# Relation layer of a fused graph network: order of layer norm, table copies, word loads and early blocks, and one-hot matrices on another engine

## The reference

```python
h = relu(layernorm(x))                        # 3125 x 128
out = h @ w_self.T
weights = einsum('rb,bio->rio', coefficients, bases)   # 16 relations from 8 bases
for r in range(16):
    msg += where(edge_type == r, h[dst] @ weights[r], 0)
out = out.at[src].add(msg)                    # 100000 edges
x = x + out
```

## Time and profile before

| | |
|---|---|
| median of 3 runs | 4468.73 us (4462.77 to 4470.12) |
| the profiled execution | 4464.81 us, of which its span 4463.1 us |
| relation layer, first instruction to end | 3338.3 to 4463.1 us |
| POOL busy | 3173.6 us (71%) |
| DVE, ACT busy | 2543.3 us (57%), 1263.6 us (28%) |
| PE busy, mean granted clock | 3091.4 us (69%), 0.686 |

### The profile page before, as it was taken

The page is one execution under the profiler, slowest core; times in us unless marked ns, Lnnn a source line. Parts: engine busy times, 40 slices in busy tenths (PEclk is TensorE's granted clock), DMA queues, the critical chain, the costliest instruction groups (busy, mean ns, idle before and its releaser), DMA issues. The chain is left out here.

```text
span 4463.1 us, 64712 instructions
## 1 busy us (share of the span) xinstructions
PE 3091.4 (69%) x17444; PEld 2321.1 (52%) x17444; DVE 2543.3 (57%) x8083; ACT 1263.6 (28%) x3878; POOL 3173.6 (71%) x3260
## 2 busy tenths in 40 slices
PE   4999999999244454454549888889878556553334
PEld 2555555556234444444448887778864333333333
DVE  6676666655456676667756666666566344431111
ACT  4333433334344444454531111111124000000000
POOL 4777777776577777777437777777764777777776
PEclk8999999999555555555555555555559787865555
DMA  4644444431334444443212223332229211211112
GB/s 98 144 94 92 94 92 94 93 87 30 105 100 108 110 106 106 106 111 103 46 46 61 74 75 79 83 88 61 56 48 283 53 52 52 53 50 50 49 49 60
DMA packets 422722, 372.59 MB, mean 83 GB/s; under 512 B 287296, under 2 KB 326090, under 8 KB 419035
## 3 DMA queue, kind: packets, MB, share of 16 engines
q0 software_dynamic: 103168, 178.48, 17.5%
q1 hardware_dynamic: 315736, 189.88, 15.7%
q10 hardware_dynamic: 3456, 0.01, 0.0%
HBM read 317.94 MB, written 35.47 MB: 79 GB/s over the span
## 5 line engine op out<-in xcount | busy, mean ns | idle before, releaser
L1108 POOL DMA_INDIRECT mlp_row<-tab,rec_d x806 | 784.5, 973 | 292.7 <-issue 244.4
L1108 POOL DMA_INDIRECT gat_row<-tab,rec_d x806 | 778.6, 966 | 265.6 <-issue 241.0
L1108 POOL DMA_INDIRECT att_row<-tab,rec_d x806 | 779.4, 967 | 255.7 <-issue 243.5
L1643 POOL DMA_INDIRECT rel_row<-tab,words_in x758 | 754.4, 995 | 231.0 <-issue 230.4
L1731 PE MATMUL rel_ps_acc<-rel_row,rel_hot 128*128 128x128 f32 x1516 | 341.7, 395 | 493.3 <-DMA rel_row<-tab,words_in 465.8
L1731 PEld LDWEIGHTS rel_ps_acc<-rel_row,rel_hot 128*128 128x128 f32 x1516 | 290.7, 285 | 618.8 <-issue 618.8
L2093 PE MATMUL gat_ps_sum<-gat_row,gat_hot 128*128 128x136 f32 x1612 | 408.3, 429 | 273.7 <-DVE gat_row L2164 250.1
L2323 PE MATMUL att_ps_sum<-att_row,att_hot 128*128 128x136 f32 x1612 | 432.8, 448 | 109.6 <-DVE acc L1485 105.1
L2093 PEld LDWEIGHTS gat_ps_sum<-gat_row,gat_hot 128*128 128x128 f32 x1612 | 352.1, 312 | 298.4 <-issue 262.8
L2323 PEld LDWEIGHTS att_ps_sum<-att_row,att_hot 128*128 128x128 f32 x1612 | 368.3, 325 | 187.1 <-DVE acc L1485 182.7
L1826 DVE TENSOR_TENSOR rel_hot<-iota,rel_local 128x512 f32<-128x512 f32 (+1 forms) x208 | 138.9, 677 | 401.0 <-PE rel_ps_acc L1731 398.0
(11 more groups left out here) (312 smaller groups left out, 5724.4 us busy)
## 6 DMA issues: line engine op xcount, KB each, us to landing
mlp_aim<-in_dst SPq DMA_DIRECT2D x195, 256.0 KB
gat_aim<-in_dst SPq DMA_DIRECT2D x195, 256.0 KB
tab<-rel_stage SPq DMA_DIRECT2D x25, 1024.0 KB, 4.8
mlp_row<-in_edge_attr SPq DMA_DIRECT2D x390, 64.0 KB, 3.0
mlp_row<-tab,rec_d POOLq DMA_INDIRECT x806
gat_row<-tab,rec_d POOLq DMA_INDIRECT x806, 2.6
att_row<-tab,rec_d POOLq DMA_INDIRECT x806
rel_row<-tab,words_in POOLq DMA_INDIRECT x758, 2.5
```

Of the source, the lines that this page charges most:

```text
L1108: gp.indirect_dma_start(row[b][:, t, :], None, table, bass.IndirectOffsetOnAxis(offsets(order[k], t), axis=0)).then_inc(s_g[b], 16)
L1643: gp.indirect_dma_start(row[r % UNROLL][:, t, :], None, tables, bass.IndirectOffsetOnAxis(g.index[:, at:at + 1], axis=0)).then_inc(s_g[r % ...
```

## The change

In neutral terms, part by part:

- **Attention bias.** `residual` no longer adds it (L887). Nine additions (`add_bias`) go in front of the extra steps of the third layer.
- **Layer norm.** DVE does the norm of all nine groups without a table copy between them. ACT copies all four parts of bins 0 to 3, and does two groups of `deviation` and `apply` behind each bin (`scaled`). From bin 4 on ACT copies parts 0 and 2, DVE parts 1 and 3. SP stores `tabh` at a = 1, 2 and 4.
- **Word loads.** SP loads run 0 at the start, runs 1 and 2 behind the stores of bins 20 and 22, and the coefficients, the bases and runs 3 to 12 behind the last store of the table.
- **Early blocks.** 16 instead of 12; the last four lie in `g.H`, and POOL waits before them until PE has transposed all groups (`s_t`).
- **Shares.** `early_coefs` runs behind the table and the first three `decode`, in two halves of 512 columns; its operand `one` lies in PSUM (`p_x`). PE waits for it (`s_mix`) before the first `chunk`, no longer for `s_in` before the products with `w_self`.
- **One-hot.** ACT makes it: a Square of (node number minus column) for each tile, and a Relu of one minus that over the block. DVE does ACT's copy to `turned`.

```diff
@@ -883,9 +883,6 @@
-            if self.layer == 3:
-                v.tensor_tensor(g.X[:, here, :], g.X[:, here, :],
-                                g.bias2[:].unsqueeze(1).broadcast_to([P, len(THREE[n]), D]), ALU.add)
@@ -1498,9 +1495,10 @@
...
-EARLY = 12
+EARLY = 16
...
+FOR_NORM = 4
@@ -1518,7 +1516,7 @@
 def by_vector(a, part):
-    return part == 3 or part == 1 and a >= len(THREE) - 2
+    return a >= FOR_NORM and part % 2 == 1
 def copies(vector, a, part):
@@ -1527,23 +1525,25 @@
     return sum(by_vector(*divmod(n, 4)) == vector for n in range(4 * a + part + 1))
-def early_coefs(v, ch, g, spare, kind_i, kind, coef, s_in):
...
+def early_coefs(v, ch, g, one, prod, kind_i, kind, coef, s_in):
+    word, most = g.word[:, 0:EARLY * TILES], EARLY * TILES // 2
+    wide = [P, most, N_REL]
+    one, prod = (x.rearrange("p (t r) -> p t r", r=N_REL) for x in (one, prod))
+    per_base = coef[:].rearrange("p (r b) -> p b r", b=N_BASES)
+    ch.do(v.tensor_scalar(kind_i[:], word, INDEX_BIT, N_REL - 1, ALU.logical_shift_right, ALU.bitwise_and))
+    ch.do(v.tensor_copy(kind[:], kind_i[:]))
+    ch.do(v.tensor_single_scalar(kind[:], kind[:], 1.0, ALU.add))
     v.wait_ge(s_in, 32)
...
+    for n in range(2):
+        here = slice(n * most, (n + 1) * most)
+        ch.do(v.tensor_tensor(one, g.iota[:, 0:N_REL].unsqueeze(1).broadcast_to(wide),
+                              kind[:, here].unsqueeze(2).broadcast_to(wide), ALU.is_equal))
+        for b in range(N_BASES):
+            ch.do(v.tensor_tensor(prod, one, per_base[:, b].unsqueeze(1).broadcast_to(wide), ALU.mult))
+            ch.do(v.tensor_reduce(g.mixes[:, here, b], prod, AX.X, ALU.add))
 def relation(nc, g, args, tables, out):
@@ -1567,15 +1567,14 @@
         number, local = c.sb("number", [P, HALF_TILES * N_HALVES], I32), c.sb("local", [P, HALF_TILES * N_HALVES])
...
-        homes = [g.TMP[:].rearrange("p a f -> p (a f)"), g.acc[:].rearrange("p a f -> p (a f)")]
-        half = EARLY // 2
-        early = [homes[o // half][:, o % half * BLOCK:(o % half + 1) * BLOCK].rearrange("p (t f) -> p t f", t=TILES)
+        homes = [home[:].rearrange("p a f -> p (a f)") for home in (g.TMP, g.acc, g.H)]
+        each = N_ROWS // BLOCK
+        early = [homes[o // each][:, o % each * BLOCK:(o % each + 1) * BLOCK].rearrange("p (t f) -> p t f", t=TILES)
                  for o in range(EARLY)]
...
@@ -1598,21 +1597,27 @@
         @block.sync
         def _(sp):
-            for n in runs:
+            def words(n):
                 sp.dma_start(*word_run(g, n)).then_inc(s_word[n], 16)
-            sp.dma_start(bases[:], args["bases"].rearrange("b i o -> i b o")).then_inc(s_in, 16)
-            sp.dma_start(coef[:], args["coefficients"].rearrange("r b -> (r b)").partition_broadcast(P)).then_inc(s_in, 16)
+            words(0)
             by_node = g.tabh.rearrange("(a n) f -> n a f", a=N_BINS)
             by_bin = tables.rearrange("(a n r) f -> a n (r f)", a=N_BINS, n=P)
             for a in range(N_BINS):
-                if a in (2, 5, 7):
-                    n = (2, 5, 7).index(a)
+                if a in (1, 2, 4):
+                    n = (1, 2, 4).index(a)
                     here = slice(THREE[3 * n][0], THREE[3 * n + 2][-1] + 1)
                     sp.wait_ge(norm.s_h, 3 * n + 3)
                     sp.dma_start(by_node[:, here, :], g.H[:, here, :]).then_inc(s_row, 16)
-                sp.wait_ge(s_mc, copies(True, a, 3))
+                ge(sp, s_mc, copies(True, a, 3))
                 sp.wait_ge(s_ma, copies(False, a, 3))
                 sp.dma_start(by_bin[a], stage[:, a % ring, :]).then_inc(s_out[a % ring], 16)
+                if a in (20, 22):
+                    words((20, 22).index(a) + 1)
+            sp.dma_start(coef[:], args["coefficients"].rearrange("r b -> (r b)").partition_broadcast(P)).then_inc(s_in, 16)
+            sp.dma_start(bases[:], args["bases"].rearrange("b i o -> i b o")).then_inc(s_in, 16)
+            for n in runs[3:]:
+                words(n)
@@ -1628,6 +1633,8 @@
             gp.wait_ge(s_node_i, 1)
             gp.wait_ge(s_row, 48)
             for o in range(EARLY):
+                if o == 2 * each:
+                    gp.wait_ge(s_t, len(THREE))
                 for t in range(TILES):
                     at = o * TILES + t
                     gp.indirect_dma_start(early[o][:, t, :], None, g.tabh,
@@ -1646,10 +1653,16 @@
         @block.scalar
         def _(act):
-            norm.deviation(act, 0)
-            norm.apply(act, 0)
-            keep_three(act, ht, p_t, 0, s_t, s_tc)
-            norm.deviation(act, 1)
+            def scaled(n):
+                if n < len(THREE):
+                    norm.deviation(act, n)
+                if 0 < n <= len(THREE):
+                    norm.apply(act, n - 1)
+            for n in range(3):
+                scaled(n)
+                if n == 1:
+                    keep_three(act, ht, p_t, 0, s_t, s_tc)
             for a in range(N_BINS):
                 if a >= ring:
                     act.wait_ge(s_out[a % ring], 16 * (a // ring))
@@ -1657,10 +1670,8 @@
                     if not by_vector(a, part):
                         act.wait_ge(s_m, banks * a + part + 1)
                         act.copy(stage[:, a % ring, part * 512:(part + 1) * 512], p_m[part]).then_inc(s_ma, 1)
-                if a + 2 < len(THREE):
-                    norm.deviation(act, a + 2)
-                if a + 1 < len(THREE):
-                    norm.apply(act, a + 1)
+                scaled(2 * a + 3)
+                scaled(2 * a + 4)
                 if a % 3 == 1 and a // 3 + 1 < len(THREE):
                     keep_three(act, ht, p_t, a // 3 + 1, s_t, s_tc)
             act.wait_ge(s_tabs, 1)
@@ -1670,11 +1681,26 @@
                     at = (2 * o + h) * HALF_TILES
                     act.dma_start(g.word[:, at:at + 1], g.words_dram[bass.ds(start, P)].rearrange("(p t) -> p t", t=1)
                                   ).then_inc(s_word[-1], 16)
-            for e in range(EARLY):
-                act.wait_ge(s_chunk, CHUNKS * e + 1)
-                if e >= 2:
-                    act.wait_ge(s_part, (CHUNKS - 1) * (e - 1))
-                act.copy(turned[:, e % 2, :], p_x[:]).then_inc(s_turned, 1)
+            def measure_gap(k):
+                o = ORDER[k]
+                ge(act, s_sum, k - (HOTS - 1))
+                act.wait_ge(s_loc, decoded(o))
+                for t in real_tiles(o):
+                    at = o * TILES + t
+                    ins = act.activation(hot[k % HOTS][:, t, :], g.iota[:], ACT.Square, scale=-1.0, bias=local[:, at:at + 1])
+                ins.then_inc(s_gap, 1)
+            def make_hot(k):
+                act.wait_ge(s_gap, k + 1)
+                there = hot[k % HOTS][:, tile_slice(ORDER[k]), :]
+                act.activation(there, there, ACT.Relu, scale=-1.0, bias=1.0).then_inc(s_hot, 1)
+            for k in range(N_BLOCKS + 1):
+                if k < N_BLOCKS:
+                    measure_gap(k)
+                if k:
+                    make_hot(k - 1)
         @block.tensor
         def _(pe):
@@ -1707,7 +1733,6 @@
             pe.wait_ge(s_mc, copies(True, N_BINS - 1, 3))
             pe.wait_ge(s_ma, copies(False, N_BINS - 1, 3))
             pe.wait_ge(s_tabs, 1)
-            pe.wait_ge(s_in, 32)
             for a in range(N_BINS):
                 pe.matmul(p_acc[:, a * D:(a + 1) * D], ht[:, a * P:(a + 1) * P], g.w_self[:],
                           start=(a % 4 == 0), stop=True, skip_group_check=True)
@@ -1751,6 +1776,9 @@
             for k in range(N_BLOCKS):
                 mm_sum(k)
+                if k == CHUNKS_AT:
+                    pe.wait_ge(s_in, 32)
+                    pe.wait_ge(s_mix, 1)
                 if 0 <= k - CHUNKS_AT < CHUNKS * EARLY:
                     chunk(k - CHUNKS_AT)
@@ -1760,29 +1788,18 @@
             v.wait_ge(s_w, 1)
             v.tensor_copy(g.w_self[:], p_m[3][:, 0:D]).then_inc(s_wc, 1)
             norm.begin(v)
-            norm.residual(v, 0)
-            norm.scan(v, 0)
-            norm.residual(v, 1)
-            norm.scales(v, 0)
-            norm.scan(v, 1)
+            for n in range(len(THREE)):
+                norm.residual(v, n)
+                if n:
+                    norm.scales(v, n - 1)
+                norm.scan(v, n)
+            norm.scales(v, len(THREE) - 1)
             v.wait_ge(s_word[0], 16)
             v.tensor_scalar(node_i[:], g.word[:, 0:EARLY * TILES], INDEX_BIT + 4, 0xFFF, ALU.logical_shift_right,
                             ALU.bitwise_and).then_inc(s_node_i, 1)
-            def tables_s():
-                yield from source_tables(v, ch, g, sort, turn, bins_f, s_cnt)
-                v.sem_inc(s_tabs, 1)
-                yield from early_coefs(v, ch, g, spare, kind_i, kind, coef, s_in)
-            later = tables_s()
+            later = source_tables(v, ch, g, sort, turn, bins_f, s_cnt)
             for a in range(N_BINS):
-                n = a + 2
```

(27 more changed lines are left out.)

20 lines of the change are left out of this document (removed).

## The result

The changed kernel takes 4404.45 us (median of 4 runs, 4400.82 to 4405.87), the kernel before 4469.42 us in runs beside it (4 runs, 4462.77 to 4473.07). The ratio is 0.9856, with a 95% interval from 0.9845 to 0.9868: 65 us faster. The forecast was 4406 us in a range of 4394 to 4430. The profiled execution took 4400.82 us, of which the span 4399.1; the sum had given 4404.9 and 4403.2.

A forecast was written before the change was run, and what follows sets the result against it. POOL's gather queue bounds the relation layer. 14.0 us at the start plus 10.0 and 37.2 of stretching, less a 2.2 wait, cut the span from 4463.1 to 4403.2, hence 4406 us, range 4394 to 4430.

The forecast's parts named there:

- T: Start of the layer norm's first division: 3341.0 before the change, forecast at 3346.3 us.
- The border: End of the third layer: extra steps and nine bias additions start the relation layer 5.3 us later.
- 0.55 / 1.25 of cases: Third layer: share of the nine bias additions said to meet a gather's start, each costing some 0.3 us, 1.2 in all.
- The front: Layer norm to first gather on h: h complete at T + 30.1, first gather at T + 35.2, gain 14.0 us.
- Early gathers: Gathers on h: 48, a 2.2 us wait for PE's transposes, 16 more to T + 117.3; table stored with 2 us spare.
- Stretching: Gathers held by DVE instructions with two SBUF inputs: 10.0 us into acc goes, 38.7 us from the table falls to 1.5.
- Shares late, hidden: Shares computed behind the table, done at T + 142; POOL's ring would stop it only at T + 197, so no cost.
- The end: Last gather ends at T + 1044.5 (4390.8), then 12.4 us of last sums and stores make a span of 4403.2 us.
- Stretching has another cause: Rival on gathers: DVE's comparisons only share the block rhythm, so 38.7 and 10.0 us stay, 4453 us; chance 0.04.
- The table sets the start: Rival at the first table gathers: slower PE clock or queued words delay the table 8 to 20 us, 4414 to 4426; chance 0.16.
- Nothing of the front shows: Rival on the layer's start: h ready no earlier since ACT has more to do, 4420 us; chance 0.04.
- ACT's one-hots decide: Rival in the table gathers: from 4.4 us a block ACT sets the end; at 5 us, 4528 us; chance 0.03.

The follow-up runs named there:

- shares_sbuf_2: Changed kernel with the shares' operand in SBUF (an emptied stage buffer) in place of PSUM; one run, 4414.93 us.
- words_ahead: Changed kernel with all 13 runs of words loaded at the head of SP's queue again; 4412.58 us, ratio 0.9867 to the kernel before.
- bias_in_norm: Changed kernel with the attention bias added in the layer norm again, not in the third layer; one run, 4405.42 us.
- act_hot_alone_2: Kernel before with only the one-hots moved to ACT and the copy to turned to DVE; 4433.77 us, ratio 0.9902 to the kernel before.
- dve_hot_2: Changed kernel with the one-hots made by DVE again, both inputs in SBUF; 4442.36 us, ratio 0.9926 to the kernel before.

## Why the prediction was right

Every step can be read relative to T.

- **The border.** Forecast 5.3 us later (4.1 for steps behind the loop, 1.2 for additions that hold gathers), measured 2.3 (3343.33 less 3341.0). The steps were right: from POOL's last gather of the third layer to SP's first instruction of the next it is 4.4 us more than before (14.37 against 9.98). The 1.2 us was wrong. The nine additions fall from 2376 to 2416 us, and the longest gather there takes 0.97 us: each addition ended before the next gather began or at most 0.16 us after, since they follow POOL's rhythm and don't fall at random in it. "0.55 / 1.25 of cases" was the step that failed. The third layer's last gather ended 2.1 us earlier, which no part of the sum foresaw; in shares_sbuf_2, whose third layer is the same, it began 4.6 us later. The last gathers, before and after:

```profile
3327.36 0.94 POOL L1108 DMA_INDIRECT att_row<-tab,rec_d  x1 [0.30 <-issue]
```

```profile
3324.87 1.36 POOL L1105 DMA_INDIRECT att_row<-tab,rec_d  x1 [0.30 <-issue]
```

- **The front.** First gather on h at T + 35.7, forecast T + 35.2. Before it was T + 54.5 (3395.48 less 3341.0), so the front gained 18.8 us by itself; 4.4 went to the border, and the wait for h fell by 14.4. The words' part is shown (first gather at T + 44.6 in words_ahead, 8.9 us later). The other 9.9 are the order of norm and copies by difference, and bias_in_norm puts 2.75 of them down to the bias.
- **Early gathers.** Wait for the transposes 1.5 us, forecast 2.2; first table gather at T + 117.1, forecast T + 117.3. The table's margin is 4.6 us, forecast 2.
- **Stretching.** 10.0 us of the gathers into acc: 0.2 left. 38.7 us of the table gathers: about 0.3 left, forecast 1.5. The causes were shown one at a time: the one-hots' move gave 37.5 us on the kernel before (act_hot_alone_2) and 28.8 on the changed one (dve_hot_2), the shares' operand in PSUM gave 8.5 (shares_sbuf_2). The shares' new place alone would not have done: of the 10.0 us taken from the gathers into acc, 8.5 would have come back in the table gathers.
- **Shares late, hidden.** The sixteen pairs end at 3490.5, T + 147, forecast T + 142; one pair takes 1.07 + 0.69 us. POOL never waits for a buffer (no PE in the group's idle time).
- **The end.** The last gather ends at 4386.7, T + 1043.4, forecast T + 1044.5; 12.4 us to the end of the span as before. 4403.2 forecast less 3.0 of the border and 1.1 of the rest is 4399.1.

The rivals. *Stretching has another cause* is out: the same instruction holds a gather or not by where its operand lies (shares_sbuf_2). The page "SBUF — State Buffer" of the Trainium skill, section "Who interferes with whom", says that `tensor_tensor` was not seen to stall descriptor generation; for these indirect gathers the runs show the opposite (983 against 944 ns), and with its other sentence, that a DVE instruction with two SBUF inputs contends with a GpSimd instruction that reads SBUF, they agree. *The table sets the start* is out in the changed kernel, by 4.6 us, and shown to be near: with twelve blocks it is what happens. PE's granted clock from 3355 to 3450 us was 1.00 (2.4 GHz), so its products didn't slow down, on which that rival had rested. *Nothing of the front shows* is out: h was ready at T + 29.8 and gathered from T + 35.7. *ACT's one-hots decide* is out: 1.84 us a block against the 4.4 that it would take.

What was luck: the forecast knew nothing of the chips that hold back transfers. On one of them it would have been wrong by far, with the same kernel.

## What to carry to other kernels

If one engine's queue is nearly the whole chain, add up what its instructions take above their undisturbed time, and look at which instruction of another engine was under way each time one was long: 51 ns on 758 gathers were worth more than the reordering of the layer's front. Before moving such work to another engine, try its operands: one input in PSUM leaves the gathers alone. A scalar pointer in place of a whole tensor doesn't, but four short instructions in place of a long one cut the loss (949 against 975 ns). A start that waits for a transfer is read in the queue in front of it: 29 us of small loads, needed much later, stood ahead of the store that everything waited for.

## What the runs showed of the hardware that was not expected

- **Chips differ by 17%.** The kernel before takes 4469 to 4477 us (medians) in three sets of runs and 5211 and 5213 us on two other chips. Each of those was used in one sitting, so whether it is a lasting trait of the chip isn't shown. On those, gathers of 64 KB follow each other at 1.43 us (46 GB/s) from 4400 to 4800 us, though POOL's own time for one is the same 944 ns, and a change that shortens POOL's time gives 0.3% where it gives 1.4% elsewhere. What holds the transfers back there is open.
- **What holds a gather is the kind of instruction and the place of its inputs, not that DVE works or where the output lies.** `tensor_tensor` with both inputs in SBUF: 1.26 to 2.23 us, also with the output in PSUM (L1542). `tensor_scalar` with a pointer, from SBUF to SBUF: 1.01 us under one of 0.28 us and 1.43 under one of 0.75. A `tensor_tensor` with one input in PSUM, or a reduction: 0.94 us.
- **The gather resumes at a fixed distance.** It ends 0.81 to 0.83 us after DVE does, for instructions of 0.69, 1.08 and 1.55 us. As it takes 0.94 us undisturbed, DVE's last 0.12 us under it cost nothing. If it begins within some 0.04 us of DVE's start it isn't held, and the comparison takes 0.72 to 0.77 us in place of 0.69 (ten times in dve_hot_2).
